# A later place on GpSimd for image 1's row differences and for two sets of weight sums

## What is computed

```python
x = x + deformable(_gn(x), ...)     # block 0
x = x + two_convs(_gn(x), ...)      # block 1
# _gn: group norm, 32 groups of 4 channels, no weights

# deformable: a 3x3 conv gives 27 channels (9 offsets in y, 9 in x, 9 masks); x is sampled
# bilinearly at the 9 shifted places of each pixel, times the mask; then
out = einsum('bckhw,ock->bohw', sampled, weight) + bias
# and a group norm over 16 groups of 8 channels, with gamma and beta

# two_convs:
q1 = ternary_quantize(w1)                           # -1, 0, 1
out1 = relu(batchnorm(conv3x3(x, q1), gamma1, beta1))
q2 = ternary_quantize(w2)
out2 = batchnorm(conv3x3(out1, q2), gamma2, beta2)
return relu(out1 + out2)
```

## Time and profile before

| | us |
|---|---|
| median of 3 runs | 279.92 |
| lowest and highest | 279.54, 280.6 |
| the profiled execution | 280.03 |
| its span, first to last instruction | 278.3 |
| TensorE busy | 239.4 (86%) |
| VectorE busy | 217.7 (78%) |
| ScalarE busy | 172.6 (62%) |
| GpSimd busy | 169.6 (61%) |

### The profile page before, as it was taken

One profiled execution on the slowest core, in us unless ns is written; L12 is line 12 of the kernel. 1 busy time (PEld: TensorE's weight loads), 2 busy tenths in 40 slices (PEclk: granted clock), 3 DMA queues, 4 the chain that ended last, 5 costly groups with the idle time before them and its releaser, 6 DMA issues.

```text
span 278.3 us, 5550 instructions
## 1 busy us (share of the span) xinstructions
PE 239.4 (86%) x1932; PEld 206.1 (74%) x1932; DVE 217.7 (78%) x472; ACT 172.6 (62%) x364; POOL 169.6 (61%) x218
## 2 busy tenths in 40 slices
PE   1599988899989999998998979899998995999900
PEld 1477757799978899897998869899965774777600
DVE  4589545989888999569978789986598777799293
ACT  2469666979768978878799876885016406631040
POOL 8120499999687678776759999387460001945042
PEclk9999999999999999999999999999999998999975
DMA  7914776543443332333323333300000000000016
GB/s 206 392 46 145 221 258 237 162 150 131 137 140 107 127 99 79 107 114 115 104 76 107 114 117 112 101 19 0 2 0 0 2 1 0 0 0 2 5 42 265
DMA packets 25593, 28.13 MB, mean 101 GB/s; under 512 B 2509, under 2 KB 23613, under 8 KB 25560
## 3 DMA queue, kind: packets, MB, share of 16 engines
q1 hardware_dynamic: 24912, 25.95, 28.6%
q10 hardware_dynamic: 648, 1.76, 1.7%
HBM read 19.87 MB, written 6.78 MB: 96 GB/s over the span
## 4 chain that ended last, share of the span: by engine, by line
PE 57%; DVE 24%; ACT 8%; issue 4%; DMA 3%; POOL 1%; SPq 1%; POOLq 0%; DVEq 0%
PE PS L940 11%; PE PS L847 6%; PE PS L975 6%; PE PS L849 5%; PE PS L848 5%; PE PS L800 4%; DVE slo L1543 4%; PE PS L829 4%; PE PS L830 4%; PE PS L831 4%; DVE vlo L1554 4%; PE PS L729 3%; ACT vhi L1153 2%; DVE st L1442 2%; DMA xs<-in_x 2%
## 5 line engine op out<-in xcount | busy, mean ns | idle before, releaser
L583 POOL TENSOR_TENSOR vt<-rowm,hat 128x1026 f32<-128x1026 f32 x36 | 70.8, 1966 | 24.0 <-PE PS L809 22.3
L1554 DVE TENSOR_TENSOR vlo<-PS,vhi 128x576 fp32r<-128x576 f32 (+2 forms) x88 | 50.0, 590 | 17.0 <-ACT vhi L1153 16.6
L1153 ACT ACTIVATE vhi<-PS 128x576 fp32r<-128x576 f32 (+2 forms) x88 | 43.9, 525 | 18.6 <-PE PS L831 18.4
L1543 DVE TENSOR_TENSOR slo<-PS,shi 114x512 fp32r<-114x512 f32 (+1 forms) x68 | 43.2, 675 | 6.2 <-ACT shi L1141 6.1
L847 PE MATMUL PS<-vhi,wdhi 128*128 128x256 f32 x144 | 43.6, 303 | 1.1 <-ACT xb L1160 1.1
L829 PE MATMUL PS<-shi,patch 114*128 114x288 f32 (+1 forms) x136 | 42.6, 313 | 1.3 <-DVE vlo L1554 0.9
L849 PE MATMUL PS<-vhi,wdlo 128*128 128x256 f32 x144 | 40.5, 281 | 0.0
L848 PE MATMUL PS<-vlo,wdhi 128*128 128x256 f32 x144 | 40.5, 281 | 0.0
L830 PE MATMUL PS<-slo,patch 114*128 114x288 f32 (+1 forms) x136 | 40.2, 295 | 0.0
L831 PE MATMUL PS<-shi,patch 114*128 114x288 f32 (+1 forms) x136 | 40.0, 294 | 0.0
L1141 ACT ACTIVATE shi<-PS 114x512 fp32r<-114x512 f32 (+1 forms) x68 | 36.8, 593 | 4.0 <-PE PS L800 3.5
(11 more groups left out here) (212 smaller groups left out, 517.3 us busy)
## 6 DMA issues: line engine op xcount, KB each, us to landing
patch<-xt SPq DMA_DIRECT2D x136, 114.0 KB
xt<-xtv SPq DMA_DIRECT2D x4, 1024.0 KB, 6.3
xs<-in_x SPq DMA_DIRECT2D x3, 512.0 KB, 8.3
wraw<-in_L_conv_w SPq DMA_DIRECT2D x2, 576.0 KB, 10.4
out<-xb SPq DMA_DIRECT2D x4, 256.0 KB, 2.6
wd_raw<-in_L_conv_weight ACTq DMA_DIRECT2D x1, 576.0 KB, 7.6
xs<-in_x SPq DMA_DIRECT2D x2, 256.0 KB, 4.4
omr<-omr SPq DMA_DIRECT2D x8, 64.0 KB, 4.5
```

Of the source, the lines that this page charges most:

```text
L583: g.tensor_tensor(vt[:, n % 2, :, :].rearrange("p t (r j) -> p t r j", r=WR), rowm[:, n % 2, :, :].unsqueeze(3).to_broadcast([P, TAPS, WR, ...
L1153: last = a.activation(places(vhi), src, ACT.Copy)
L1543: d.tensor_tensor(lo, src, hi, ALU.subtract).then_inc(slo_ok, 1 if pairs(n) == 2 else 3)
L1554: last = d.tensor_tensor(places(vlo), src, places(vhi), ALU.subtract)
```

## The change

On GpSimd, `point_differences(0)` moves from pass 27 of the loop to pass 33, right behind the last outer product, where `point_weights(0)` stood. `point_weights(0)` moves behind the loop and behind `point_differences(1)`. `point_weights(1)` gets a wait in front of it, for the residuals of both images of conv1 (`wl_ok` 4). On ScalarE, `point_heads(0, 0)` and `point_heads(0, 1)` move from slots 31 and 32 to slots 34 and 35. On VectorE, one of the two `point_tails(1, m)` moves behind `deviation(GN1, B - 1)`, and TensorE's mean of squares that waits for this deviation moves from behind the fifth to behind the seventh matmul of `conv_points(1)`. No operation is added or taken away.

```diff
@@ GpSimd, the loop @@
-                if n == 33:
-                    point_weights(0)
+                if n == CHUNKS - 3:
+                    point_differences(0)
                 if n >= CH and n % CH in (7, 8):
                     add_y(n // CH - 1, n % CH - 7)
-                if n == CH * 3:
-                    point_differences(0)
 
             point_differences(1)
+            point_weights(0)
             pool.wait_ge(y_done, 1)
             g.memset(point_edges(vsp[:, :]), 0.0).then_inc(vpad, 1)
             g.memset(r1p[:, :, 0:W], 0.0).then_inc(vpad, 1)
             g.memset(r1p[:, :, W + HW:ROWS * W], 0.0).then_inc(vpad, 1)
+            pool.wait_ge(wl_ok, 2 * NW)
             point_weights(1)
@@ TensorE, convolutions() @@
-                conv_points(1, ((5, group_square, GN1, B - 1),))
+                conv_points(1, ((7, group_square, GN1, B - 1),))
@@ ScalarE, beside(n) @@
-                    if n == CH * (b + 2) + 4:
-                        heads(GN1, 0) if b == 0 else point_heads(0, 0)
-                    if n == CH * (b + 2) + 5:
-                        whole(GN1, 0) if b == 0 else point_heads(0, 1)
+                    if b == 0 and n == CH * 2 + 4:
+                        heads(GN1, 0)
+                    if b == 0 and n == CH * 2 + 5:
+                        whole(GN1, 0)
+                if n in (CHUNKS - 2, CHUNKS - 1):
+                    point_heads(0, n - CHUNKS + 2)
@@ VectorE, finish() @@
-                for m in range(2):
-                    point_tails(1, m)
+                point_tails(1, 0)
                 deviation(GN1, B - 1)
+                point_tails(1, 1)
```

## The result

The changed kernel took 275.47 us, the median of 4 runs from 274.91 to 276.24. The kernel before, with one more run beside it, has a median of 279.73. The ratio is 0.9846, with a 95% interval of 0.9811 to 0.9882. With its repeat the changed kernel stands at 276.18 (10 runs), at the lower end of the range, and the kernel before at 279.58 (the 77 runs beside the later sets), which is 3.4 us; why the first four lie lower is the subject of much of what follows. A ratio is made from the runs that lie close to a kernel's fastest and a median from all of them, so the two can differ where the runs scatter.

A forecast was written before the change was run, and what follows sets the result against it. TensorE was taken as the bound, with its idle time before VectorE's small instructions to win. 280.03 less 1.3 (loop) and 1.6 (tail) gives 277.1, the median 0.1 lower: 277.0 us; range 276.2 to 278.9.

The forecast's parts named there:

- The loop's part: Sampling loop, slot 29: moving image 1's differences frees L1393 and removes TensorE's idle time; 1.3 us, bounds 0 to 1.41.
- the collision at 175.58: Loop, L1428 at 176.89 before: follows a product TensorE itself releases, so it stays and gives nothing.
- The covers of parts 1 and 2: Loop: GpSimd's moved differences and ScalarE's moved heads hide behind other waits and nine conv1 matmuls; cost 0, uncovered heads 0.5 us.
- The rival that the loop's gain is used up: Slot 29's own waits take the loop's 1.3 us, leaving only the tail: 278.4 us, chance 0.13.
- The tail's part: Behind the loop: later conv2 weight sums and the reordered deviation bring conv1 of image 3 sooner; 1.6 us, bounds 1.4 to 1.85.
- capped by TensorE's square mean: Behind the loop, GN8: VectorE's variance can't be before 205.67, so it gains 1.44 us in place of 2.0.
- The GN1 chain: Behind the loop: sums run beside VectorE's GN1 steps; L1428 first, or held up to 1.00 and TensorE stands 0.1 to 0.2.
- The rival with the full catch: Held sums delay L1428 and two steps behind it, TensorE stands 0.9 us; tail gain 0.8, 277.9 us, chance 0.13.
- The deviation beside L602: Behind the loop: L1393 at 199.25 takes 0.22 us beside GpSimd's L602; if held, the gain is 0.3 less.
- the sum: Whole kernel: profiled 280.03 less 1.3 and 1.6 gives 277.1; the median 0.1 lower, 277.0 us.
- The sign "from the third image's head to the end the same distances as before": From image 3's head to the kernel's end: unchanged distances would show the forecast right.

## Why the prediction missed

**The loop's part was right.** Predicted 1.3; slot 31's turn came 1.31 sooner, 1.22 of it by the edit. L1395 took the 0.22 that was predicted, nothing new ended last in slot 29, and the collision at 175.58 stayed as it was said to. The covers of parts 1 and 2 held: ScalarE's heads stand in the new slots, and no wait of TensorE came of them. The rival that the loop's gain is used up has fallen; a loss of that size does happen when the weight sums stay in the loop.

**The tail's part was right in kind and 0.2 low.** Predicted 1.6 with bounds 1.4 to 1.85. The batch norm's aggregate came at 230.16 before and at 227.08 after, 3.08 sooner; less the 1.31 at slot 31's turn this is 1.77. That VectorE would be capped by TensorE's square mean showed as the 0.56 of idle time before L1414 at 204.35. The GN1 chain was caught by the third addition, in one instruction of 0.88 us, and cost TensorE 0.24 where up to 0.2 was said. It was not the instruction that the prediction asked about: L1428 did come first, as L1430 at 214.76 and with its 0.22, and the next one was held (L1433 before, L1435 after). The rival with the full catch (0.9) has fallen.

**The deviation beside L602** took 0.22 (197.94 beside 197.61 to 198.79), as the row of before had it. The Trainium skill, "SBUF — State Buffer", section "Who interferes with whom", would have it held; at this place the trace disagrees. A small instruction closer behind L602's start does take longer: in the changed kernel with the old order of the tails L1435 began at 215.26, 0.15 us behind L602 (215.11), and took 0.37 in place of 0.16. For the memset the same section says that it holds nobody, and there the trace agrees: L1587 took 1.23 beside L650.

**The step that failed is the sum.** It started from the profiled execution, 280.03 us, and took from it only what the change moves. That execution had 3.4 us of half clock at conv2's start, and I had counted them in without seeing them: the stretches that I read for the granted clock end at 216 us, and the page's row of the clock in 40 slices was read for the loop alone. A granted clock of 0.50 from 234 to 237 us was there to be read. So no term, no rival and neither end of the range had the clock in it. Its absence was worth 1.46 us in the profile after; taken from the forecast of 277.0 it gives 275.5, which is where the first four runs lie. The sign "from the third image's head to the end the same distances as before" is the one that failed in that profile: up to conv2's first matmul it held (12.19 us before, 12.26 after), and the 18 matmuls behind it were 1.46 shorter.

How much of the measured 4.3 us is then the change's? The work is 3.0 us by the traces (1.22 and 1.77) and 2.8 by the lowest runs with the matmuls. The mean clock of each run fits: span times (1 - mean clock) is what a run lost to it, if roughly. It doesn't say where, and in the profiles about 5 to 6 us of it lie behind TensorE's last matmul, where it costs nothing. Runs that lost 6.5 to 7.8 us have medians of 278.58 before (23 runs) and 275.35 after (5), 3.2 apart; runs that lost 8 to 9 have 279.70 (37) and 276.65 (5), 3.1 apart. These groups are not clean: the profiled execution of before lost 7.0 us, with the slow stretch at conv2's start and none near 46 us, and took 280.03, 1.45 over the median of its group. So the group seems to hold runs whose slow stretch lay where it costs nothing. On top of the work comes the clock. 17 of 77 runs of the kernel before lost 10 us or more and none of 10 after, but so did 4 of 12 with the loop's edit and the weight sums behind the loop, so 10 us is no sign of the stretch at 166 us. A loss of 12 us is a better one: the profile that had it 6.8 us long at 166, at conv2's start and near 46 us lost 12.3. 9 of the 77 runs lost that much, and none of the 54 runs of the five kernels with the loop's edit and without the matmuls. All runs together give 3.4. The other 0.9 us of the first four runs is chance between executions: the same kernel gave 276.46 in the next set. That this chance lay at conv2's start in all four is not shown, since only one of them has a trace.

What stays open is why an execution falls into the slow stretch and another does not. At 3.40 us of idle time it came 8 times of 9, at 1.4 us 4 times of 6, at unchanged work. The Trainium skill, "TensorE: Matmul & The Clock Gate", section "What's actually happening", says that the number of slow matmuls at a kernel's start differs between runs of one kernel; the traces here show the like in its middle. There is also a slow stretch near 46 us in 10 of the 14 profiles. It cost TensorE nothing that shows: the turn of slot 26 came between 156.71 and 157.43 us in these, and between 156.97 and 157.52 in the three without it. In the one profile left the stretch lies near 40 us and the turn came at 157.86. Nothing was tried on it.

## What to carry to other kernels

Read the granted clock of every stretch of the profile of before, to its end, and put each slow stretch into the sum as a term of its own, which may go or come with any edit that touches the idle time ahead of it. An idle time of TensorE then has two prices: its own length, and the half clock that may follow it. When GpSimd's work is moved away from one small VectorE instruction, list what it lies over next; here the loop's move gained nothing until the weight sums had left the loop too, and the wait moved the sums onto VectorE's next small instruction (0.93 us in place of 0.22) until VectorE's order was changed with it. To share a gain out between two edits, run each without the other and measure from one landmark of the trace to another that lies ahead of a slow stretch.

## What was unexpected in the hardware

- TensorE at half clock for 3.4 us, or for 6.8, at an idle time of 3.40 us and even at one of 1.4. The price was 1.4 to 2.6 us at conv2's start (18 matmuls in 5.92 to 7.14 us for 4.57), and 1.0 or 2.4 us in the loop.
- Thirteen matmuls that nobody reads, in 3.15 us of idle time, made a kernel 1.7 to 2.0 us faster.
- The delay between GpSimd and VectorE goes both ways: GpSimd's addition of 384 elements took 1.88 us beside an instruction of VectorE that took 1.91 for 1.23. Side by side they took turns.
